# A graph network and experts on one core: 17 chunks a block and one shared chunk for five blocks

## The reference

```
h   = layernorm(x)
s   = h @ W1
a   = segment_sum(s[dst] * w, by src) + s
r   = relu(batchnorm(a) * gamma + beta)
t   = r @ W2
g   = segment_sum(t[dst] * w, by src) + t
x1  = x + g
out = x1 + moe(layernorm(x1))      # 8 experts, 2 of them per token, gelu, 256 wide
```

## Time and profile before

| what | us |
|---|---|
| median of three runs | 5008.68 |
| span of the profiled execution | 4551.4 |
| the profiled execution's own time | not shown beside its span |
| PE busy | 3882.9 (85%) |
| DVE busy | 3658.9 (80%) |
| ACT busy | 3272.1 (72%) |
| POOL busy | 3001.4 (66%) |
| gathers of the last stage (L1284), 1620 of the 1800 | 1591.1 busy, 982 ns each |

### The profile page before, as it was taken

One profiled execution on the slowest core, in us unless ns is written; L12 is line 12 of the kernel. 1 busy time (PEld: TensorE's weight loads), 2 busy tenths in 40 slices (PEclk: granted clock), 3 DMA queues, 4 the chain that ended last, 5 costly groups with the idle time before them and its releaser, 6 DMA issues.

```text
span 4551.4 us, 89101 instructions
## 1 busy us (share of the span) xinstructions
PE 3882.9 (85%) x28087; PEld 3392.1 (75%) x28087; DVE 3658.9 (80%) x10176; ACT 3272.1 (72%) x6937; POOL 3001.4 (66%) x3177
## 2 busy tenths in 40 slices
PE   1688888888889989985689988998889988998998
PEld 1688888888767777774468877887777877887788
DVE  8799888989778888885568878878787888877786
ACT  3799988989978778774466666666666666666665
POOL 0466766767656566653777777777777777777751
PEclk7799999999999999996579999999999999999999
DMA  7788888888799899976434444444444444444431
GB/s 226 277 324 327 324 324 326 325 317 304 274 334 325 316 333 324 328 270 183 132 108 124 119 116 121 116 126 116 121 117 126 117 119 120 121 122 116 114 98 36
DMA packets 323817, 928.86 MB, mean 204 GB/s; under 512 B 50896, under 2 KB 132896, under 8 KB 320848
## 3 DMA queue, kind: packets, MB, share of 16 engines
q0 software_dynamic: 153216, 483.15, 32.3%
q1 hardware_dynamic: 167960, 426.60, 28.7%
q10 hardware_dynamic: 2172, 13.35, 0.8%
HBM read 597.06 MB, written 325.83 MB: 203 GB/s over the span
## 4 chain that ended last, share of the span: by engine, by line
PE 36%; DVE 20%; DMA 14%; ACT 11%; issue 9%; POOL 8%; SPq 1%; ACTq 0%; DVEq 0%; POOLq 0%
PE ps L1433 7%; DMA X<-h,tabT 7%; POOL X L1284 6%; PE ps L1454 5%; DMA msgd<-A,tabT 4%; DVE S L1194 3%; PE ps L1230 3%; PE ps L1323 3%; ACT A L868 3%; DVE low L1198 2%; DMA L<-msgd 2%; PE ps L772 2%; PE ps L803 2%; PE ps L1013 2%; PE ps L1327 2%
## 5 line engine op out<-in xcount | busy, mean ns | idle before, releaser
L1284 POOL DMA_INDIRECT X<-h,tabT x1620 | 1591.1, 982 | 597.5 <-issue 384.2
L1312 ACT ACTIVATE gH<-X,tabT 128x256 fp32r<-128x256 f32 x1080 | 529.1, 505 | 471.5 <-DMA X<-h,tabT 449.6
L868 ACT ACTIVATE A<-ps,A 128x256 f32<-128x256 f32 x1856 | 741.8, 514 | 76.2 <-PE ps L804 74.0
L917 POOL DMA_INDIRECT msgd<-A,tabT x464 | 573.5, 1236 | 327.4 <-ACT A L868 248.1
L1301 DVE SCALAR_TENSOR_TENSOR gL<-X,tabT,gH 128x256 fp32r<-128x256 f32 x1080 | 518.5, 480 | 192.5 <-ACT gH L1312 190.9
L1296 DVE TENSOR_SCALAR s<-iota,tabT 128x125 fp32r<-128x125 f32 x1800 | 577.1, 338 | 0.8
L803 PE MATMUL ps<-winH,DT 128*128 128x256 f32 x1856 | 508.1, 306 | 51.3 <-issue 32.3
L1325 PE MATMUL ps<-gH,s 128*125 128x256 f32 x1200 | 400.4, 335 | 111.5 <-ACT gH L1312 84.8
L804 PE MATMUL ps<-winL,DT 128*128 128x256 f32 x1856 | 468.5, 285 | 0.0
L1323 PE MATMUL ps<-X,s 128*125 128x256 f32 x1080 | 365.0, 422 | 119.7 <-ACT X L1308 67.6
L803 PEld LDWEIGHTS ps<-winH,DT 128*128 128x128 f32 x1856 | 358.5, 193 | 68.6 <-issue 44.4
(11 more groups left out here) (274 smaller groups left out, 11009.6 us busy)
## 6 DMA issues: line engine op xcount, KB each, us to landing
L<-msgd SPq DMA_DIRECT2D x200, 650.0 KB, 6.2
L<-msgd SPq DMA_DIRECT2D x200, 520.0 KB, 6.1
A<-sbd SPq DMA_DIRECT2D x58, 805.0 KB, 6.5
msgd<-A SPq DMA_DIRECT2D x100, 390.0 KB
X<-h,tabT POOLq DMA_INDIRECT x1620, 2.8
winR<-h SPq DMA_DIRECT2D x116, 128.0 KB
A<-in_x SPq DMA_DIRECT2D x10, 1120.0 KB
h<-A ACTq DMA_DIRECT2D x10, 1120.0 KB
```

Of the source, the lines that this page charges most:

```text
L868: e.activation(M[:, n, 0:F], psum[4 + v % 4][:, (n % 2) * F:(n % 2 + 1) * F], ACT.Identity, scale=M[:, n, F + 2:F + 3]).then_inc(evc, 1)
L917: e.indirect_dma_start(msgd, bass.IndirectOffsetOnAxis(ap=idxI[g % 4][:, t:t + 1], axis=0), msg[g % 3][:, t * 4 * RW:(t + 1) * 4 * RW], No ...
L1284: e.indirect_dma_start(B.G[c % GRL], None, h2, bass.IndirectOffsetOnAxis(ap=tab3[:, c, 0:1].bitcast(I32), axis=0)).then_inc(gatl[c % GRL], 16)
L1312: e.activation(B.gH[c % HR2][:, :], B.G[c % GRL], ACT.Identity, scale=w_).then_inc(g_hi, 1)
```

## The change

Each block's own part has KM = 17 chunks, 2176 places, now laid as (place // 17, place % 17) and loaded as 5, 4, 4, 4 chunks. The room in `msgd` stays 18 chunks a block, and so do the scatter and the fills. What lies beyond 2176 places, of TB = 5 blocks together, is one chunk of at most 128 places ("tail"); there are NT = 20. Their row numbers in `msgd` (`tailX`) are worked out on chip by DVE (`dve_tails`, after the verdict's first sum, with one small matmul for a running sum over blocks); a tail place beyond the five blocks' need points to a row of zeros (`ZROW`). If five blocks need more than 128 places, the general branch is taken. POOL fetches a tail with an indirect DMA in the read stage, and again in the last stage from h2. Each of the five blocks adds the same tail chunk with its own selection (`tailD` holds each place's node plus 125 for each block of distance), so PE still has 18 chunks a block, the tail's always split. Zeros are stored at the start in the room before and behind the blocks in `msgd` too.

```diff
-NCF = NB * KC
+KM = KC - 1
+TB = 5
+NT = NB // TB
+NMF = NB * KM
+NCF = NMF + NT
+MAIN = KM * P
-PIECES = [(b, k, n) for b in range(NB) for k, n in ((0, 5), (5, 4), (9, 5), (14, 4))]
+PIECES = [(b, k, n) for b in range(NB) for k, n in ((0, 5), (5, 4), (9, 4), (13, 4))]
@@ sp_begin, after the first loads of x @@
+            e.wait_ge(cst, 7)
+            for r0 in (0, RMAX):
+                e.dma_start(msgd[r0:r0 + PADN, :].rearrange("(p k) r -> p k r", p=P),
+                            zrow[:, 0:RW].rearrange("p (o r) -> p o r", o=1).broadcast_to([P, PADN // P, RW])).then_inc(fillm, 16)
+            e.dma_start(msgd[RMAX + PADN:ZROW + 1, :], zrow[0:ZROW + 1 - RMAX - PADN, 0:RW]).then_inc(fillm, 16)
@@ dve_verdict: dve_tails(e, own), its longest chain @@
+            own.done(e.tensor_scalar(tailN, base[:, G2:G2 + 1], float(-MAIN), 0.0, ALU.add, ALU.max))
+            e.tensor_scalar(tailL, lowT[0:NB, 0:NB + 1], tailN, None, ALU.mult).then_inc(vio, 1)
+            e.wait_ge(vsum, 2)
+            own.done(e.tensor_copy(tailP, psum[0][:, 16:16 + NB + 1]))
...
+            own.done(e.tensor_reduce(tailW, tailD[0:1, :], AX.X, ALU.max))
...
+            own.done(e.tensor_scalar(tailX, tailS, float(ZROW), None, ALU.add))
...
+            own.done(e.scalar_tensor_tensor(groups(tailD), each(tailS), -1.0, steps(tail125), ALU.mult, ALU.add))
@@ pe_verdict @@
+            e.wait_ge(vio, 2)
+            e.matmul(psum[0][:, 16:16 + NB + 1], ones[0:NB, :], tailL, start=True, stop=True).then_inc(vsum, 1)
@@ act_read @@
+            def tail(j):
+                e.wait_ge(t_gat[j % 2], 16 * (G2 + j // 2 + 1))
+                if j >= 2:
+                    e.wait_ge(r_mm, 4 * TB * (j - 1))
+                e.activation(B.tailH[j % 2][:, :], B.tail[j % 2][:, 0:F], ACT.Copy).then_inc(t_hi, 1)
+                if k == PC and b % TB == 0:
+                    tail(b // TB)
@@ pool_read @@
+            def fetch(j):
+                if j >= 2:
+                    e.wait_ge(r_mm, 4 * TB * (j - 1))
+                    e.wait_ge(r_tab, tabs_upto(4 * TB * (j - 2) + 1))
+                e.indirect_dma_start(B.tail[j % 2][:, :], None, msgd, bass.IndirectOffsetOnAxis(ap=tailX[:, j:j + 1], axis=0)
+                                     ).then_inc(t_gat[j % 2], 16)
+            fetch(0)
+            fetch(1)
+                if k == 0 and b % TB == 2 and 2 <= b // TB + 1 < NT:
+                    fetch(b // TB + 1)
@@ dve_read @@
+                own.done(e.tensor_scalar(d, d, T[:, F + 1:F + 2], None, ALU.add))
+                e.wait_ge(t_hi, j + 1)
+                e.tensor_tensor(B.tailL[j % 2][:, 0:F], T[:, 0:F], B.tailH[j % 2][:, :].bitcast(F32), ALU.subtract).then_inc(t_sel, 1)
+            def tail_select(b):
+                e.tensor_scalar(B.tailS[b % 2][:, :].rearrange("p (a b) -> p a b", b=5), B.iota, tailD[:, b:b + 1], None,
+                                ALU.is_equal).then_inc(t_sel, 1)
@@ pe_read, after a block's last piece @@
+                    e.wait_ge(t_hi, b // TB + 1)
+                    e.wait_ge(t_sel, tails_upto(b))
+                    e.matmul(psum[q][0:R, 0:F], Ts, B.tailH[b // TB % 2][:, :], start=False, stop=False)
+                    m = e.matmul(psum[q][0:R, 0:F], Ts, B.tailL[b // TB % 2][:, 0:F], start=False, stop=True)
@@ pool_last @@
+            def tail(j):
+                if j >= 2:
+                    e.wait_ge(g_mm, TB * KC * (j - 1))
+                e.indirect_dma_start(B.tailG[j % 2], None, h2, bass.IndirectOffsetOnAxis(ap=tab3[:, NMF + j, 0:1].bitcast(I32), axis=0)
+                                     ).then_inc(t_gat[j % 2], 16)
-            for c in range(NCF):
+            for c in range(NMF):
+                if c % (TB * KM) == 4:
+                    tail(c // (TB * KM))
                 gather(c)
@@ act_prepare, at a block's 18th tick (k == KM) @@
+            if k == KM:
+                if b % TB == 0:
+                    e.wait_ge(t_gat[j % 2], 16 * (G2 + NT // 2 + j // 2 + 1))
+                    if j >= 2:
+                        e.wait_ge(g_mm, TB * KC * (j - 1))
+                    e.activation(B.tailH[j % 2][:, :], B.tailG[j % 2], ACT.Identity, scale=tab3[:, NMF + j, 2:3]).then_inc(t_hi, 1)
+                return
```

More of the change, by code:

```diff
@@ L48 @@
 RMAX = PADN + (NB - 1) * STRIDE + KC * P
+ZROW = RMAX + PADN + 8
+NDUMP = 3
 GFILL = 92
@@ L243, in build @@
         lowT = cut(P)
+        tailL = small[0:NB, 842:842 + NB + 1]
         onesb = cut(P // 2).bitcast(BF16)
@@ L295, in build @@
         bn = small[:, 530:570]
+        tailP = small[:, 640:640 + NB + 1]
+        tailO = small[:, 742:742 + NB]
+        tailI = small[:, 842:842 + NB]
+        tailV = small[:, 316:316 + NB]
+        tailD = small[:, 420:420 + NB]
+        tailS = small[:, 6:6 + NT]
+        tailX = small[:, 26:26 + NT].bitcast(I32)
+        tail125 = small[:, 46:46 + TB]
+        tailN = small[0:NB, 52:53]
+        tailW = small[0:1, 76:77]
         phase.close()
@@ L356, in build @@
         idxr = sem_1("idxr")
-        gatl = gat + [sem_1(f"gat{k}") for k in range(GR, GRL)]
+        t_gat = scat[0:2]
+        t_hi, t_sel = sem_1("t_hi"), sem_1("t_sel")
+        gatl = gat + [sem_1(f"gat{k}") for k in range(GR, GRL - 2)] + scat[2:4]
         one_way.close()
@@ L981, in dve_verdict @@
             own.done(e.tensor_reduce(flagf, psum[0][0:1, 0:8], AX.X, ALU.add))
+            dve_tails(e, own)
+            ready()
+            own.done(e.tensor_tensor(flagf, flagf, tailW, ALU.add))
             if force is not None:
@@ L1105, in __init__ @@
                     self.L = [first.enter_context(nc.sbuf_tensor(f"L{i}", [P, PC * RW], F32)) for i in range(LR)]
+                    self.tail = [first.enter_context(nc.sbuf_tensor(f"tail{i}", [P, RW], F32)) for i in range(2)]
                 self.low = [st(f"low{i}", PC * RW, FR) for i in range(LR)]
+                self.tailL = [st(f"tailL{i}", RW, FR) for i in range(2)]
+                self.tailH = [st(f"tailH{i}", F, FR) for i in range(2)]
+                self.tailS = [st(f"tailS{i}", R, FR) for i in range(2)]
                 self.mH = [st(f"mH{i}", PC * F, FR) for i in range(HR)]
@@ L1178, in pool_read @@
                 selected(e, u)
-                e.tensor_copy(tab3[:, b * KC + k:b * KC + k + n, :], L3[:, :, F:F + 3]).then_inc(r_tab, 1)
+                e.tensor_copy(tab3[:, b * KM + k:b * KM + k + n, :], L3[:, :, F:F + 3]).then_inc(r_tab, 1)
+                if k == PC and b % TB == 0:
+                    j = b // TB
+                    e.wait_ge(t_gat[j % 2], 16 * (G2 + j // 2 + 1))
+                    e.tensor_copy(tab3[:, NMF + j, :], B.tail[j % 2][:, F:F + 3]).then_inc(r_tab, 1)
         def dve_read(e, B, own):
@@ L1203, in dve_read @@
                     parts(u + 2)
-                if k + n == KC:
+                if k == PC:
+                    if b % TB == 0:
+                        tail(b // TB)
+                    tail_select(b)
+                if k + n == KM:
                     e.wait_ge(r_mm, u + 1)
@@ L1252, in __init__ @@
                 self.gL = [split(f"gL{i}", F) for i in range(HR2)]
+                self.tailH, self.tailL = ([split(f"gt{p}{i}", F) for i in range(2)] for p in "HL")
+                self.tailG = [t[:, :].bitcast(F32) for t in self.tailL]
                 self.Zb = [cut(1024, R) for i in range(4)]
@@ L1326, in pe_chunk @@
                 e.wait_ge(g_lo, split_upto(c, whole2))
-                m = e.matmul(psum[q][0:R, 0:F], Sc, B.gL[c % HR2][:, :], start=False, stop=k == KC - 1)
+                m = e.matmul(psum[q][0:R, 0:F], Sc, B.gL[c % HR2][:, :], start=False, stop=False)
             m.then_inc(g_mm, 1)
```

123 lines of the change are left out of this document (97 added, 26 removed).

## The result

| | us |
|---|---|
| kernel before, beside the changed one | 5013.02 (5002.78 to 5025.06, 4 runs) |
| changed kernel | 4934.44 (4921.05 to 4941.61, 4 runs) |
| ratio | 0.9836, interval 0.9817 to 0.9855 |
| predicted | 4896.7 (4866 to 4942) |

Faster by 79 us where 112 were forecast; the time is in the range, but outside the forecast's own 4885 to 4910. Page and stage windows after (columns as in the earlier trace rows); the windows run from the read stage's first matmul to its last, and from the first gather to the last.

The account below looks back on a forecast made before the run. The prediction took POOL's issue of gathers to bound the last stage up to 4250 us, and the read stage to be near two limits, DMA and engines. -95 - 18 + 1 = -112 us, so 5008.7 - 112 = 4896.7 us, range 4866 to 4942.

Parts of the forecast that it names:

- rival A: Last stage: the consumers (PE) take over, so it gives 48 us; total -65, 4944 us; chance 0.14.
- Last stage, -95 us: POOL's issue of gathers bounds it until 4250 us; 74 fewer gathers there at 1.285 us each save 95 us.
- Its sign: Rival A's sign in the last stage: gaps before gathers ended by PE before 4100 us.
- Read stage, -18 us: Read stage: 10.6 MB less to load, 33 us if DMA bound, 0 if engines bind; the middle, 18, taken.
- rival B: Read stage DMA bound, and the last stage's end follows the gathers too: 33 + 103 = -136, 4873 us; chance 0.12.
- rival C: Read stage gives nothing, DVE and PE bind between the bursts: -94, 4915 us; chance 0.20.
- +10 - 22 + 12 = 0: DVE, read stage: 31 more selections +10 us, 69 fewer chunks of low -22, 20 tails +12.
- Verdict, 0: Before the flag: 3.8 to 6.2 us of DVE work, about 0.5 for PE, under DVE's 7.95 us idle; cost nothing.
- Start, +1: Zero stores in SP's queue: 2.6 us to issue, 13 us of DMA, covered; between 0 and 13 us, 1 taken.
- The 457 us: Median of the runs above the profiled execution's span of 4551.4 us; taken as lying around the span, unchanged.
- Rival D: Tail fetches crowd one row and delay landings behind them, 20 times per stage; at 5 us each +88, 5097 us; chance 0.04.

Follow-up runs that it names:

- e2: Changed kernel whose third piece of each block loads five chunks again, four of them used: 4889.68 us, 0.9809 of the kernel before.
- e1: Changed kernel with 80 more gathers in the last stage into a buffer nobody reads, 1800 again: 4987.37 us, 1.0003 of the kernel before.
- e0: The kernel before, unedited, profiled a second time: 4983.08 us.
- e6: Changed kernel without 567 of TensorE's low matmuls (even blocks, last stage), on the faster kind of chip: 4468.62 us, 0.9783 of the kernel before.
- e10: Same edit to the changed kernel as e6, on the slower kind of chip: 4919.65 us, 0.9824 of the kernel before.
- e4_after: The changed kernel, unedited, on the faster kind of chip: 4470.3 us, 0.9779 of the kernel before.
- e7: Changed kernel whose read stage fetches the tails but does not add them: 4904.85 us, 0.9797 of the kernel before.
- e3: Kernel before with every fourth round of 20 gathers left out, old rows used (1360 gathers): 4730.97 us, 0.948 of the kernel before.
- e8_tb25: Changed kernel with one shared chunk for 25 blocks instead of five, 1704 gathers in the last stage: 4443.55 us, 0.9724 of the kernel before.

## Why the prediction was right

**The number: in part luck.** The forecast's -112 us stood for the trace's kind of chip, but was taken from times of the other. On that kind of chip the change gave -99.5 us; the forecast has the last stage's part of it right and the read stage's wrong. On the chip of its own times it gave -79, nearer to rival A's -65 than to -112: the time lies in the range because the range was widened for rival A (4944).

**Last stage, -95 us: right in size and mechanism on the trace's kind of chip.** There the stage went from 2352 to 2260 us, 92 / 80 = 1.15 us a gather (99.5 / 80 = 1.24 of the total); on the other 1.22 of the total between e2 and e1, and 0.98 in the changed kernel's own comparison (78.6 / 80). Its stages differ by 2744 - 2683 = 61 us, but across two chips; on one chip, e0 against e2, by 95. The five executions with 1720 gathers there lie between 2647 and 2683, so 61 to 97. On this other kind the path was not the forecast's: POOL does wait, for TensorE, and the gathers come 1.56 us apart (2683 / 1720). Why one less is still worth 1.2 us isn't shown.

**Rival A.** Its sign was there on the timed kind: gaps of 140 and 108 us ended by matmuls, long before 4100 us. Its reason was not found: 567 matmuls less change nothing on either kind (e6, e10, within their limit). TensorE stops, and it stops with the gathers: 261, 337 and 365 stops with 1360, 1800 and 1800 gathers, 328 to 378 with 1720, one with plain loads, as many with a quarter of the bytes. What is left as the source is what POOL does for an indirect gather, or that its 128 rows lie scattered in memory: the plain loads changed both, and no run tells them apart. By what way that reaches TensorE, and why one kind of chip only, is open. The instruction queues move the same on both kinds (236 packets, 3.87 MB in the larger one, in the changed kernel's trace and in e4_after's).

The Trainium skill, "DMA: Bandwidth & Descriptors", SWDGE vs HWDGE vs iDMA, says that DMAs issued from GpSimd, plain and indirect, get their descriptors from its software. The trace agrees as to the queue (q0 in both), and shows beside it that the two differ in cost, 0.54 and 0.96 us, and in what they do to TensorE.

**Read stage, -18 us: wrong, and this is the step that failed.** It became some 8 us longer instead (780, 786 and 780 before; 782, 785, 789, 790, 792, 792, 793, 793, 793 after). The 18 was the middle between bytes that bind (33) and engines that bind (0), and bytes give nothing (e2): that rules out rival B for this stage and bears out rival C as far as it went. C and the forecast both held the engines' work equal; for DVE +10 - 22 + 12 = 0. Here is what DVE did (e4_after, read stage, for the earlier trace rows):

```profile
L1310 DVE TENSOR_SCALAR S<-gap,L 128x125 fp32r<-128x125 f32 x1132 | 305.0, 330 | 20.6 <-DMA L<-msgd 20.4
L1314 DVE TENSOR_TENSOR low<-L,mH 128x768 fp32r<-128x768 f32 (+1 forms) x267 | 288.8, 1082 | 15.5 <-ACT mH L1255 15.5
L1327 DVE TENSOR_SCALAR tailS<-gap,small 128x125 fp32r<-128x125 f32 x100 | 33.3, 333 | 0.0
L1321 DVE TENSOR_TENSOR tailL<-tail,tailH 128x256 fp32r<-128x256 f32 x20 | 8.8, 439 | 0.0
L1319 DVE TENSOR_SCALAR small<-small,tail 128x5 f32<-128x5 f32 x20 | 4.8, 242 | 0.0
```

Selections 305.0 + 33.3 against 324.0: +14, of which 10 were seen. Tails 13.6, as forecast (12). The low parts 12.5 us less, not 22: the pieces of four chunks instead of five save DVE 67 chunks (the prediction has 69), but there are still 267 instructions, so a chunk saved is worth 12.5 / 67 = 0.19 us and not the 0.32 that the whole line gives. Together +15 by these lines where 0 was taken, in an engine that is in the chain; the windows give DVE only +6 (650.6 in the earlier trace rows, 656.3 in e4_after), since short instructions overlap. That it is DVE's share of the tails that lengthens the stage is argued; that the tails do is shown by e7. The bursts before L are not seen to shorten either: the pieces of L of this kind in the chain of waits are 9.8 to 14.3 us long in the kernel before and 8.8 to 13.1 in e4_after. The one at the earlier trace rows' place:

```profile
1700.51 11.51 DMA L<-msgd
```

**Verdict, 0: right.** The work for the tails, then the flag (changed kernel, DVE, against the earlier trace rows):

```profile
1286.35 0.13 DVE L1012 TENSOR_SCALAR small<-A 100x1 f32<-100x1 f32 x1
...
1291.31 0.15 DVE L1070 TENSOR_TENSOR small<-small 1x1 f32<-1x1 f32 x1
1293.80 0.14 DVE L1077 TENSOR_SCALAR small<-small 1x1 int32<-1x1 f32 x1 [2.34 <-DMA msgd<-A,tabT]
```

5.1 us (3.8 to 6.7 forecast), and still the scatter's landing ends the wait, now of 2.34 us.

**Start, +1: right in its outcome, wrong in the size of its parts.** SP's queue (changed kernel, against the earlier trace rows):

```profile
11.07 30.95 SPq L430 DMA_DIRECT2D msgd<-A  x2
42.07 10.65 SPq L432 DMA_DIRECT2D msgd<-A  x1
52.77 0.98 SPq L434 DMA_DIRECT2D sbd<-A  x1
...
150.62 2.04 SPq L974 DMA_DIRECT2D winR<-h  x3
```

The three fills hold the queue for 41.6 us, not 2.6 (the small third one, of 9 rows, for 10.65), and the store of sbd goes out at 52.8 instead of 14.6. The first window of h1 still starts at 150.6, as before: DVE was the cover, and it is much longer than was known.

**Around the span.** The 457 us were the difference of two kinds of chips. As a ratio the forecast was 0.9776, and 0.9779 came out on its trace's kind of chip, but that is chance: it divides 112 us by a time of the other kind; by 4570 it is 0.9755. There the last stage's -92 and the read stage's +9 make up -83. The two traces are only 4551.4 - 4481.6 = 70 us apart, since e4_after's read stage also starts 16 us later (1276 against 1260), and e4_after's profiled execution is its slowest (4483.49 us). The change is not seen to cost anything ahead of the read stage: on one chip that stage starts at 1285 and 1293 us in the kernel before (e0, e3) and at 1286 and 1288 in the changed one (e1, e2). So the 99.5 us between the medians can't be split into stages more finely than this.

**Rival D** did not come: it needed landings that hold others up, and none was seen (e8_tb25), and the total is faster on every chip.

## What to carry to other kernels

Before a sum is laid on a trace, compare the trace's span with the times: where they differ by more than a per cent or two, the stage lengths are of another execution than the one that is timed, and neither the microseconds nor the ratio need carry over (here 0.978 on one kind of chip, 0.984 on the other). Where an engine issues gathers without waiting for anybody, its cadence times their number is the price, and fewer gathers is the change to make; here a TensorE busy for 90% beside it was not the bound. A chunk left out of an engine's loop saves only what its instructions lose in elements, and the pieces that replace it count in full.

## What was not expected of the hardware

- The same program takes 4570 us on one chip and 4984 to 5013 us on others, and nearly all of the difference lies in the stage with indirect gathers (2352 against 2744 us). With plain loads instead the two are 4279 and 4307 us.
- On the slower kind TensorE stops, mostly for about 0.7 us, about once in five gathers (337 in 1720), with nothing to wait for that the trace shows; with plain loads it has one such stop.
- A plain load of 128 x 1 KB costs POOL 0.54 us to issue, a gather of as many rows 0.96, whether of 1 KB or of 256 B a row.
- Two stores of 2.13 MB of zeros and one of 9 KB behind them hold SP's queue for 30.95 and 10.65 us; 1.28 MB loads of x just ahead of them take it 0.7 to 1.4 us, those just behind them 4.2 and 4.8.
